# A one-hot of destination nodes by edge, built by a DMA transpose instead of a comparison on VectorE

## What is computed

```python
edge_index = jnp.stack([src, dst])
x = _layernorm(x + L0(x, edge_index))            # degree-normalised sum of neighbours
x = _layernorm(x + L1(x, edge_index, edge_attr, edge_weight, node_type, node_vec, ...))

# L0: row, col = src, dst (and self loops)
norm = deg_inv_sqrt[row] * deg_inv_sqrt[col]
out = segment_sum(label_mat[row] * norm[:, None], col)

# L1
gate = silu(edge_attr @ W1.T + b1) @ W2.T + b2 + adapt_logit(emb[z[src]], emb[z[dst]])
msg = gate * h[dst] * (cw(distance) * node_mult[dst])[:, None]
agg = segment_sum(msg, src) / clip(segment_sum(node_mult[dst], src), 1e-8)
out = layernorm(h + agg) * gamma + beta
```

## Time and profile before

| | |
|---|---|
| median of 3 runs | 3067.45 us (3059.66, 3067.45, 3067.46) |
| span of the profiled execution, first to last instruction | 3050.1 us |
| around the span (median less span) | 17.4 us |
| mean granted TensorE clock | 0.848 |
| PE / PEld busy | 74% / 63% |
| DVE busy | 79% |
| POOL busy | 69% |
| ACT busy | 46% |
| DMA, mean over the span | 145 GB/s |

### The profile page before, as it was taken

The page is one execution under the profiler, slowest core; times in us unless marked ns, Lnnn a source line. Parts: engine busy times, 40 slices in busy tenths (PEclk is TensorE's granted clock), DMA queues, the critical chain, the costliest instruction groups (busy, mean ns, idle before and its releaser), DMA issues. The chain is left out here.

```text
span 3050.1 us, 73627 instructions
## 1 busy us (share of the span) xinstructions
PE 2251.7 (74%) x25909; PEld 1913.8 (63%) x25909; DVE 2404.4 (79%) x5424; ACT 1399.4 (46%) x2929; POOL 2117.9 (69%) x1852
## 2 busy tenths in 40 slices
PE   6970477678787787777787878787878788876674
PEld 5860366566666675666676767676666666665664
DVE  9994577778787787877788788888888888875886
ACT  7982244444444454444444444444444444444122
POOL 7506777877777777777777777777777777750241
PEclk9665688888888898888888889888888988888887
DMA  8405233344434444333454444554545444452984
GB/s 314 152 7 158 61 111 112 104 119 121 117 112 119 122 125 114 113 112 114 123 155 145 144 145 145 146 147 142 158 132 163 150 155 145 143 146 81 419 327 174
DMA packets 174620, 441.51 MB, mean 145 GB/s; under 512 B 92296, under 2 KB 92296, under 8 KB 154440
## 3 DMA queue, kind: packets, MB, share of 16 engines
q1 hardware_dynamic: 103388, 236.05, 23.4%
q0 software_dynamic: 67888, 194.98, 21.9%
q10 hardware_dynamic: 3004, 5.90, 0.6%
HBM read 292.51 MB, written 144.27 MB: 143 GB/s over the span
## 5 line engine op out<-in xcount | busy, mean ns | idle before, releaser
L722 POOL DMA_INDIRECT slot<-table,gidx x1616 | 1827.3, 1131 | 617.3 <-issue 606.8
L821 PEld LDWEIGHTS route<-parts,oh_r 128*128 128x128 bf16 x11312 | 758.0, 99 | 88.9 <-issue 64.1
L821 PE MATMUL route<-parts,oh_r 128*128 128x148 bf16 x11312 | 806.4, 231 | 3.4 <-DVE parts L1224 3.0
L1089 DVE TENSOR_SCALAR oh_r<-iota_r,spot 128x896 bf16<-128x896 f16 x1616 | 613.5, 450 | 75.4 <-PE route L821 75.3
L894 ACT ACTIVATE routed<-route 128x444 bf16<-128x444 f32 (+1 forms) x1010 | 508.8, 514 | 250.2 <-PE route L821 234.8
L856 PE MATMUL pwin<-slot,oh_d 128*128 128x144 bf16 x1616 | 175.6, 284 | 424.0 <-DMA slot<-table,gidx 392.1
L856 PEld LDWEIGHTS pwin<-slot,oh_d 128*128 128x128 bf16 x1616 | 153.8, 156 | 448.6 <-issue 291.6
L777 PEld LDWEIGHTS pwin<-win,oh_t 128*128 128x128 bf16 x4848 | 258.8, 115 | 180.8 <-issue 96.1
L747 PE MATMUL phid<-attr,w 80*96 80x512 f32 x404 | 285.8, 798 | 48.6 <-issue 47.7
L777 PE MATMUL pwin<-win,oh_t 128*128 128x80 bf16 (+1 forms) x4848 | 272.6, 225 | 54.4 <-ACT ssum L904 49.4
L1195 DVE TENSOR_TENSOR prod<-slot,got 128x256 f32<-128x256 f32 x202 | 84.7, 419 | 243.1 <-ACT parts L955 243.0
(11 more groups left out here) (228 smaller groups left out, 3211.3 us busy)
## 6 DMA issues: line engine op xcount, KB each, us to landing
rows<-slots SPq DMA_DIRECT2D x51, 1295.0 KB, 10.1
oh_t<-dst_row SPq DMA_DIRECT2D x101, 512.0 KB
erows<-slots SPq DMA_DIRECT2D x51, 777.0 KB
attr<-in_edge_attr SPq DMA_DIRECT2D x101, 320.0 KB
slots<-zeros SPq DMA_DIRECT2D x53, 518.0 KB
slot<-table,gidx POOLq DMA_INDIRECT x1616
table<-tab SPq DMA_DIRECT2D x3, 676.0 KB, 6.0
weight_t<-weights SPq DMA_DIRECT2D x101, 8.0 KB
```

Source lines behind the costliest of these rows:

```text
L722: e.indirect_dma_start(out=slot[:, s, g, :], out_offset=None, in_=table0, in_offset=bass.IndirectOffsetOnAxis(ap=gidx[:, s, g:g + 1], axis ...
L821: mm = e.matmul(route[:, (NPH * m + phase) % 2, RC * (j - a):RC * (j - a + 1)], oh_r[:, c, slot_of, :], parts[:, s % 2, c, :], start=(c == ...
L1089: oh = e.tensor_scalar(oh_r[:, c], iota_r[:, :, :], spot[:, s % 2, c:c + 1], None, ALU.is_equal)
```

## The change

`oh_d` is no longer computed by VectorE. `places` moves from lag 4 to lag 0 and to the place in DVE's list where `onehots` stood; `rows`, which feeds it, moves to lag 0 and ahead of `load` in SP's list; `oh_t` gets six buffers instead of two, since it now lives from a tile's first turn to its `pick` four turns later. A new step of SP, `by_edge` (lag 1, right behind `rows`), makes `oh_d` from `oh_t` with one DMA transpose of 128 x 2048 values of bf16, SBUF to SBUF, 16 blocks of 128 x 128. It waits for `places` of the tile and for `total` of the tile two before, and `total` waits for the transpose's semaphore `dst_in` instead of `ohd`. `oh_d` is now laid out by group first, so each matmul's weights are contiguous.

```diff
-            oh_d = sb("oh_d", [P, 2, P, G], BF16, ph)
-            oh_t = sb("oh_t", [P, 2, G, P], BF16, ph)
+            oh_d = sb("oh_d", [P, 2, G, P], BF16, ph)
+            oh_t = sb("oh_t", [P, U, G, P], BF16, ph)
...
                     def rows(i, s):
                         t = U * i + s
-                        if since(i, s, 2):
-                            e.wait_ge(picked, 2 * (t - 1))
+                        if since(i, s, U):
+                            wait_apart(e, picked, 2 * (t - U + 1), passed)
...
+                    def by_edge(i, s):
+                        t = U * i + s
+                        wait_apart(e, oht, t + 1, passed)
+                        if since(i, s, 2):
+                            wait_apart(e, summed, t - 1, passed)
+                        e.dma_start_transpose(oh_d[:, s % 2], oh_t[:, s].rearrange("p g q -> p (g q)")
+                                              ).then_inc(dst_in[s % 2], 16)
...
-                        over_tiles(e, NT, U, (index, 0), (load, 4), (rows, 4), (weigh, 4),
+                        over_tiles(e, NT, U, (index, 0), (rows, 0), (by_edge, 1), (load, 4), (weigh, 4),
...
                     def total(i, s):
-                        e.wait_ge(ohd, t + 1)
+                        e.wait_ge(dst_in[s % 2], 16 * (pair_of(i, s) + 1))
...
-                            mm = e.matmul(sums, oh_d[:, s % 2, :, g],
+                            mm = e.matmul(sums, oh_d[:, s % 2, g, :],
                                           rows[:, g, :], start=(g == 0), stop=(g == G - 1))
...
-                    def onehots(i, s):
-                        t = U * i + s
-                        if since(i, s, 2):
-                            e.wait_ge(summed, t - 1)
-                        e.tensor_tensor(oh_d[:, s % 2], number[:, :, :], bc_mid(w16[:, bass.ds(t * G, G)], P),
-                                        ALU.is_equal).then_inc(ohd, 1)
...
-                                   (onehots, 0), (buckets, 4), (route_onehots(0), 5), (put_rows, 5),
+                                   (places, 0), (buckets, 4), (route_onehots(0), 5), (put_rows, 5),
                                    (add_early, 7, EARLY_FROM), (early_onehots, 6, EARLY_FROM), (less_first, 2),
-                                   (less_high(0), 5), (product(1), 5), (less_second, 2), (places, 4),
+                                   (less_high(0), 5), (product(1), 5), (less_second, 2),
```

More of the change, by code:

```diff
@@ L610, in build @@
             row_in = [sem(f"row_in{s}", ph) for s in range(2)]
-            (sx, ohd, ohb, oht, ohr, summed, taken, halved, chain, normed, win_h, win_r, win_m, win_l, win_ok,
+            dst_in = [sem(f"dst_in{s}", ph) for s in range(2)]
+            (sx, ohb, oht, ohr, summed, taken, halved, chain, normed, win_h, win_r, win_m, win_l, win_ok,
              hidden, hid_sb, ranked, placed, routing, rows_ok, picked, got_ok, gated, own, gate_used,
              val_ok, high, rested, mid, split_ok, stepped, group_rows, ones_ok) = (
-                sem(n, ph) for n in ("sx", "ohd", "ohb", "oht", "ohr", "summed_f", "taken", "halved", "chain",
+                sem(n, ph) for n in ("sx", "ohb", "oht", "ohr", "summed_f", "taken", "halved", "chain",
                                      "normed", "win_h", "win_r", "win_m", "win_l", "win_ok", "hidden", "hid_sb",
@@ L776, in step @@
                                     n = WX if k else WW
-                                    mm = e.matmul(pwin[:, g // 4, first:first + n], oh_t[:, s % 2, m * HC + g, :],
+                                    mm = e.matmul(pwin[:, g // 4, first:first + n], oh_t[:, s, m * HC + g, :],
                                                   win[:, s, AT[k]:AT[k] + n], start=(k == 0), stop=(k == 2),
@@ L1056, in places @@
                         e.wait_ge(row_in[s % 2], 16 * (pair_of(i, s) + 1))
-                        e.tensor_scalar(oh_t[:, s % 2], oh_t[:, s % 2], iota_p[:, 0:1], None, ALU.is_equal
+                        e.tensor_scalar(oh_t[:, s], oh_t[:, s], iota_p[:, 0:1], None, ALU.is_equal
                                         ).then_inc(oht, 1)
@@ L1298, in build @@
             gate = ps("gate_f", [P, 512], F32, ph)
-            (moved, io, v, begun, asked, picked, ohs, used, summed, cleared, answer, table, attr_in,
+            (moved, io, v, begun, asked, picked, ohs, used, summed, cleared, answer, attr_in,
              hidden, hid_sb, gated, asked1, picked1, split, used1, summed1, col1) = (
@@ L1302, in build @@
                     "moved", "io", "v", "begun", "asked", "picked", "ohs", "used", "summed", "cleared",
-                    "answer", "table", "attr_in", "hidden", "hid_sb", "gated", "asked1", "picked1",
+                    "answer", "attr_in", "hidden", "hid_sb", "gated", "asked1", "picked1",
                     "split", "used1", "summed1", "col1"))
@@ L1317, in _ @@
                         e.dma_start(weight[:, :], weights).then_inc(moved, 16)
-                        e.wait_ge(table, 1)
+                        e.wait_ge(cleared, 3)
                         e.dma_start(far_rows.rearrange("(h l) c -> l h c", l=P), rows[:, :, :]).then_inc(moved, 16)
@@ L1435, in _ @@
                         done(e.tensor_tensor(rows[:, :, C:TW], rows[:, :, C:TW], fixed[:, :, 2, :], ALU.add))
-                        e.nop().then_inc(table, 1)
+                        e.nop().then_inc(cleared, 1)
                         with e.Fori(0, NT) as t:
```

2 lines of the change are left out of this document (1 added, 1 removed).

## The result

| | before | after |
|---|---|---|
| median of the runs, us | 3067.45 (3059.66 to 3079.56) | 3350.09 (3342.11 to 3357.59) |
| ratio, 95% interval | | 1.092, 1.089 to 1.095 |
| span of the profiled execution | 3050.1 | 3340.3 |
| a tile, 500 to 1500 us | 24.2 | 24.3 |
| a tile, in the second half | 24.7 | 30.3 |

The account below looks back on a forecast made before the run. GpSimd's full queue was taken as the bound, not VectorE; span 3050.1 - 35 (first half) - 10 (second half) = 3005, plus 17.4 between span and median gives 3022 us, range 2988 to 3290.

Parts of the forecast that it names:

- GpSimd's queue is full, and a comparison holds up a gather: GpSimd bounds both halves; a gather issued under VectorE's comparison waits for its end, so removal frees 0.7 us a tile.
- `places` ... counts as nothing: On VectorE, places may hold a gather in its new spot but leaves its old one, so no cost was counted.
- The first half's slack for the transpose: First half: total needs the transpose 32 us later, so anything up to about 20 us is hidden by gathers.
- D: Time in which the transpose's packets move, in the path from early sum to total; taken as 3.3 us.
- the estimate by pieces: Transpose's packet time from 2048 pieces at 18 ns each over 16 engines: 2.3 us.
- A second ring of the same length as the tile: Second half: late oh_t, places, then VectorE's work to the next early sum, 24 us; no longer than the first ring.
- The slower side: The outcome that the changed kernel is slower, through a transpose too late in the second half; chance 0.43.
- late transpose: Second half: total waits for dst_in, each us of packet time beyond 3.4 costing 48 us; chance 0.43 with the block-after-block rival.
- T: Experiments' theory: the transpose itself comes too late for total; given 2 to 6 us per second-half turn in kernel 10.
- The block-after-block rival: Second half: 16 blocks each wait for the one before, transpose 24 us, time about 4025; chance 0.08 of the 0.43.
- The DMA engines fill up: Transpose traffic raises DMA share from 0.40 and 0.50 to 0.54 and 0.64; costs only with a long transpose, no own chance.
- the four signs of a wrong forecast: Second-half total waiting for the transpose, GpSimd idle over 0.30 us, SyncE's transpose row over 0.33, first-half gathers still 1.12 us.

Follow-up runs that it names:

- kernel 5: Kernel before with the comparison for oh_d cut to a copy of one column, first layer's sums left out; 3002 us, 0.979 of the kernel before.
- kernel 2: Changed kernel with oh_t's load and the transpose both issued a turn earlier, ahead of the wait for the early sum; 3155 us, 1.029 of the kernel before.
- kernel 6: Changed kernel with oh_t's load a turn ahead and the transpose behind the other loads of SyncE's turn; 3150 us, 1.031 of the kernel before.
- kernel 10: Changed kernel with only places put back at its old spot late in VectorE's turn, SyncE's list untouched; 3162 us, 1.034 of the kernel before.
- kernel 7: As kernel 6, with places also back at its old spot late in VectorE's turn, for the next tile; 3019 us, 0.988 of the kernel before.
- kernel 8: As kernel 7, with gidx's load also issued a turn earlier; 2995 us, 0.979 of the kernel before.
- kernel 4: Kernel before, comparison kept, plus one transpose per tile from a constant into a buffer nobody reads; 3200 us, 1.047 of the kernel before.
- kernel 3: Kernel before with oh_t's load, places and six buffers moved as in the change, oh_d still compared on VectorE, no transpose; 3481 us, 1.136.
- kernel 1: Changed kernel with oh_t's load alone issued a turn earlier, the transpose still behind the early sum's wait; 3161 us, 1.031 of the kernel before.

## Why the prediction was wrong

**GpSimd's queue is full, and a comparison holds up a gather.** Right. The comparison's absence gives 65 us (kernel 5), 0.64 us a tile by the gathers' mean, against the 0.7 that the prediction took. The Trainium skill (SBUF — State Buffer, Who interferes with whom) says two things of a tensor_tensor: with both inputs in SBUF it contends with GpSimd's reads there, and a probe did not see it stall DMAs. The prediction took from the second that the removal would give GpSimd nothing; kernel 5 contradicts that, and agrees with the first for gathers whose row numbers lie in SBUF.

**"`places` ... counts as nothing."** Wrong, and this is the step that lost the first half. With `places` ahead of `oh_b` a gather takes 1125 ns in the changed kernel, 1135 and 1145 in kernels 2 and 6; with `places` late in the turn it takes 1071, 1079 and 1068 in kernels 10, 7 and 8. That is some 55 ns, or 0.9 us a tile, the whole of the forecast gain. The comparison of one input that moved in costs there about what the one of two inputs that moved out had cost (1125 against 1121 ns), and in its old spot it had cost that much less. The first-half time of a tile was 24.3, not 23.5. Kernel 10, with `places` left where it was, has the forecast first half: 1071 ns (1.08 or less was the test) and 23.4 us.

**The first half's slack for the transpose.** Right: 1000 us of kernel 4 show no price at all.

**D, the transpose's packets.** Right in the middle. D was to be 3.3 us; from 1500 to 2900 us the median time from the first to the last of a transpose's 2048 packets is 3.4 us in the changed kernel. In a quiet turn it is less. Kernel 8's transpose, issued at 2118.66, has all of its packets in the DMA queues from 2119.8 to 2122.5 us (packets, MB, share of 16 engines):

```profile
q1 hardware_dynamic: 2048, 0.52, 102.4%
```

This is 2.7 us; the estimate by pieces was 2.3. But the place in which the change puts it is often not quiet. In the turn shown above the transpose's packets move from 2260.4 to 2266.3, with those of the scatter (queue 0) at the same time. From 2260 to 2266.5:

```profile
q1 hardware_dynamic: 2128, 0.67, 76.7%
q0 software_dynamic: 190, 1.01, 39.1%
```

This was 5.8 us, with the end 12.4 us behind the early sum, where the prediction had 5.0 + 3.3. The prediction took the time of each transfer from a moment in which it was alone. Of its two estimates by the Trainium skill, the one from VectorE: DVE Perf Modes, The three transpose paths (21 us for sixteen blocks of 1309 ns) is far from both numbers; the one from DMA: Bandwidth & Descriptors, Latency and other measured facts (2 us) is near the 2.7 of the quiet case.

**"A second ring of the same length as the tile ... takes no more than the first."** This is the step that failed worst. In the sum it stands as nothing, beside 10 us gained for the second half; measured, the second half lost 5.6 us a tile, some 269 us. The prediction followed `places` forward to `routes` of the next turn and found room. It did not ask who waits for what stands *behind* `places` on VectorE: `put_rows` writes `sidx` after the row of `oh_r`, and TensorE's `ranks` waits for it directly ahead of `total`. So the late load is in the path from early sum to `total` of the same turn. The size was off too: `oh_t` was to land 6.5 us behind the early sum and landed at 9.8. Measured, the path from early sum to `total` is 17.2 us in the turn shown, not 9.8. Kernel 3 shows it without any transpose, kernels 1 and 2 by taking it away.

**The rivals.** The slower side had 0.43, and its "late transpose" gives 3350 at D = 10, the very time that was measured. That is chance. `total` waited for the transpose in 7 turns of 101 (59.0 us), and the mechanism was the load. As a second wait T is real (kernel 10), at a mean of 7.6 us a turn. The block-after-block rival is out: no turn shows anything near 24 us. "The DMA engines fill up" was named only as a part of the first rival; it costs by itself (kernel 4, 1.047). The mean share alone does not tell the price: at 0.54 in the first half it was nothing, and in the second (0.71) what can be seen of it are TensorE's longer stands for its instructions and GpSimd's for `gidx`.

**What would show it.** Of the four signs of a wrong forecast three came true: SyncE's transpose row is longer than 0.33 us (median 3.4), GpSimd stands idle before gathers, and the gathers still take 1.12 us in the first half. The fourth, `total` waiting for the transpose in the second half, hardly did.

## What to carry to other kernels

When a wait moves to another place in an engine's list, walk through every instruction behind it in that turn and ask who waits for each of those, up to the end of the path. The consumer of the moved result is only one of them. Where a queue is released late and all its loads go out at once, the small ones have no time to spare, and anything that makes the release later is paid for by whoever waits for them: issue those a turn ahead, and let a new large transfer go out when the others have landed (kernel 8). And if a comparison on VectorE is removed to free a gather, check what takes its place in that spot: here the one that moved in held the gathers as much.

## What the hardware showed that was not expected

- A DMA transpose of 128 x 2048 bf16 within SBUF moves as 2048 packets of 256 bytes: 2.7 us in a quiet turn of kernel 8, 5.8 us in the turn of the changed kernel in which the scatter's packets moved too.
- Its issue holds SyncE's queue for 1.7 to 9.6 us, median 3.4, against 0.33 for a plain transfer: 8.19 us in the turn where its packets had to wait, and 2.18 in a quiet one of kernel 8. What stands behind it in that queue is late by that much.
- A load of 8 KB that was issued 0.7 us behind one of 777 KB and 1.2 us behind the start of a scatter was there only after 8.7 us (kernel 4, one turn).
- TensorE stood once in six turns until 3 us after a packet of the instruction queue: at most 4.8 us in the kernel before, up to 12.1 us where a transpose's packets moved meanwhile (kernel 4).
- A comparison with one input (`places`) held up gathers on GpSimd as one with two inputs did: its new spot costs about 0.9 us a tile more than its old one (1125 against 1071 ns a gather). And one gather lasted 5.75 us, through a row of ten comparisons.
- Where the granted clock was 0.70 to 0.75, the kernel before took more than a third longer and kernel 8 half as long again, so that it came out behind.
